# A graph network's one-hot build: edge differences on GpSimd, a re-cut load of the targets, identity and run bounds made on chip

## The reference

```python
def _L1_gnn_ref(x, edge_index, edge_attr, We, be, W1, b1, gamma, beta, W2, b2):
    msg = x[src] + (edge_attr @ We + be)
    agg = jax.ops.segment_sum(msg, dst, num_segments=x.shape[0])
    h = (agg + x) @ W1 + b1
    ...
    return h @ W2 + b2

edge_index = jnp.stack([src, dst])
x = _layernorm(x + _L0_gnn_ref(x, src, dst))
...
x = _layernorm(x + _L3_gnn_ref(x, edge_index, L3_gnn_W, L3_gnn_att_src, L3_gnn_att_dst, L3_gnn_bias))
```

## Time and profile before

| | us |
|---|---|
| median of 3 runs (1216.16 to 1217.31) | 1216.74 |
| profiled execution, its own time | 1217.54 |
| its span, first to last instruction | 1215.7 |
| PE busy in it | 1083.8 |
| DVE busy | 862.8 |
| ACT busy | 640.8 |
| POOL busy | 60.4 |

### The profile page before, as it was taken

One profiled execution on the slowest core, in us unless ns is written; L12 is line 12 of the kernel. 1 busy time (PEld: TensorE's weight loads), 2 busy tenths in 40 slices (PEclk: granted clock), 3 DMA queues, 4 the chain that ended last, 5 costly groups with the idle time before them and its releaser, 6 DMA issues.

```text
span 1215.7 us, 38923 instructions
## 1 busy us (share of the span) xinstructions
PE 1083.8 (89%) x16039; PEld 995.7 (82%) x16039; DVE 862.8 (71%) x2304; ACT 640.8 (53%) x1171; POOL 60.4 (5%) x109
## 2 busy tenths in 40 slices
PE   2766667679999999999998999599999999999997
PEld 1666656679999999999954999488989888898996
DVE  3999999975344434443631635788899899899997
ACT  1677777730000000000112402689899999999997
POOL 1000000001111111111000002000000000000000
PEclk8899999989999999999999799699999999999999
DMA  4555555410000000000000000000000000000000
GB/s 77 73 75 76 71 75 76 62 38 3 2 3 3 2 3 2 3 2 3 2 1 1 2 3 2 2 2 2 2 2 2 2 2 2 2 2 2 8 13 13
DMA packets 133045, 21.77 MB, mean 18 GB/s; under 512 B 132255, under 2 KB 132639, under 8 KB 132892
## 3 DMA queue, kind: packets, MB, share of 16 engines
q1 hardware_dynamic: 128920, 18.88, 10.3%
q10 hardware_dynamic: 3972, 0.68, 0.3%
HBM read 18.74 MB, written 0.80 MB: 16 GB/s over the span
## 4 chain that ended last, share of the span: by engine, by line
PE 55%; DVE 15%; ACT 6%; issue 3%; ACTq 0%; POOL 0%; DVEq 0%
PE bank L1927 33%; PE bank L2055 9%; DVE Mr L1537 5%; ACT Mr L922 4%; PE bank L2051 4%; PE bank L1870 3%; PE bank L1862 2%; PE bank L2115 1%; DVE F L1437 1%; DVE Mr L1544 1%; PE bank L1854 1%; DVE Nr L1500 1%; ACT F L862 1%; PE bank L1897 1%; ACT r L899 1%
## 5 line engine op out<-in xcount | busy, mean ns | idle before, releaser
L1927 PE MATMUL bank<-GH,C 128*128 128x128 f16 x7100 | 397.9, 219 | 0.0
L1927 PEld LDWEIGHTS bank<-GH,C 128*128 128x128 f16 x7100 | 396.9, 98 | 0.1
L2055 PE MATMUL bank<-F,Mr 128*128 128x260 f16 (+1 forms) x2538 | 317.4, 261 | 6.6 <-DVE Mr L1537 5.4
L2055 PEld LDWEIGHTS bank<-F,Mr 128*128 128x128 f16 x2538 | 214.6, 98 | 28.4 <-DVE Mr L1537 5.5
L1537 DVE TENSOR_TENSOR Mr<-Mr,C 128x640 f16<-128x640 f16 x461 | 210.8, 488 | 35.8 <-ACT Mr L922 31.8
L764 ACT ACTIVATE plo<-bank 128x256 f32<-128x256 f32 (+1 forms) x84 | 30.1, 360 | 362.9 <-PE bank L1927 346.7
L2051 PE MATMUL bank<-FN,C 128*128 128x130 f16 x1945 | 187.1, 220 | 5.3 <-DVE r L1446 4.9
L1745 PE MATMUL bank<-ohk,ohp 128*128 128x100 f16 (+3 forms) x1452 | 114.1, 214 | 81.9 <-ACT C L725 35.8
L1181 DVE TENSOR_TENSOR S<-bank,plo 128x256 f32<-128x256 f32 (+1 forms) x84 | 33.2, 395 | 209.3 <-ACT plo L764 209.2
L922 ACT ACTIVATE Mr<-cold,eaT 128x640 f16<-128x640 f32 x231 | 173.0, 819 | 11.4 <-PE bank L2055 10.5
L922 ACT ACTIVATE Mr<-eaT 128x640 f16<-128x640 f32 x230 | 172.4, 818 | 10.1 <-PE bank L2055 9.1
(11 more groups left out here) (263 smaller groups left out, 1006.5 us busy)
## 6 DMA issues: line engine op xcount, KB each, us to landing
raw<-in_edges_dram SPq DMA_DIRECT2D x237, 68.0 KB, 2.2
xs<-in_x_dram SPq DMA_DIRECT2D x1, 800.0 KB, 4.3
out_dram<-xs SPq DMA_DIRECT2D x4, 160.0 KB
dsts<-in_dst_dram SPq DMA_DIRECT2D x1, 465.0 KB
raw<-in_edges_dram ACTq DMA_DIRECT2D x5, 68.0 KB, 3.1
cold<-in_L_gnn_W_dram ACTq DMA_DIRECT2D x2, 64.0 KB
z<-in_L_gnn_att_src_dram SPq DMA_DIRECT2D x1, 128.0 KB, 2.8
z<-in_L_gnn_att_dst_dram SPq DMA_DIRECT2D x1, 128.0 KB, 3.0
```

Of the source, the lines that this page charges most:

```text
L1927: last = pe.matmul(bank[:, b, jj * 2 * D:(jj + 1) * 2 * D], C[:, t, (t0 + jj) * P:(t0 + jj + 1) * P], GH[:, par, t, :], start=t == 0 and j ...
L2055: return pe.matmul(bank[:, k, a_:z_], Mr[:, mi % RB, j * P:(j + 1) * P], F[:, t, a_:z_], start=start, stop=t == T - 1)
```

## The change

Five edits, all before the first hop. The differences `rest` leave DVE for a loop of their own on GpSimd, in the same order (this group's second half, then the next one's first), each waiting for the high parts (`s_hi`) alone. The 124 lines of targets are loaded as 64, 12 (SP) and 48 (ACT). The 17 parameter loads move from the front of ACT's queue to SP's, behind the loop that loads edges. `wlo` is made by two products of `bound` with a one on PE and a copy on DVE, and `ident` by a comparison on DVE. ACT runs a small activation at its front, and PE's first `begin` comes one row earlier.

```diff
@@ block.sync
-            sp.dma_start(dsts[1:RP, :], bass.AP(dst.tensor, dst.offset + (RC - 1) * ROW, [[RC * ROW, RP - 1], [1, (RC + 1) * ROW]])).then_inc(s_first, 16)
+            sp.dma_start(dsts[1:65, :], lines(1, 65)).then_inc(s_first, 16)
+            sp.dma_start(dsts[113:RP, :], lines(113, RP)).then_inc(s_first, 16)
             sp.dma_start(dsts[0:1, ROW:], dst.rearrange("(p c) -> p c", c=RC * ROW)[0:1, :]).then_inc(s_first, 16)
...
...
+                sp.dma_start(o_, i_).then_inc(s_w, 16)
+            for j_, i_ in enumerate((b1, gamma, beta)):
+                sp.dma_start(vecs[:, j_:j_ + 1], i_[:, None]).then_inc(s_w, 16)
             sp.wait_ge(s_lo, (G - 1) * 2)
@@ block.gpsimd
-            pool.iota(wlo[:], pattern=[[P * W, 2]], base=0, channel_multiplier=W, allow_small_or_imprecise_dtypes=True).then_inc(s_iota, 1)
-            pool.memset(ident, 0.0).then_inc(s_g, 1)
...
-            pool.affine_select(out=ident, in_=ident, compare_op=ALU.not_equal, fill=1.0, base=0, pattern=[[-1, P]], channel_multiplier=1).then_inc(s_cst, 1)
...
+            pool.wait_ge(s_ident, 1)
+            pool.tensor_copy(ident16, ident).then_inc(s_cst, 1)
...
+            def rest(i, k, u):
+
+                w0, w1_ = HALVES[u]
+                pool.wait_ge(s_hi, i * 4 + (k * 2 + u + 1))
+                pool.tensor_tensor(attrs(k % 2, w0, w1_), attrs(k % 2, w0, w1_), eahl[:, w0 * K:w1_ * K, 0:DE], ALU.subtract).then_inc(s_dif, 1)
+
+            rest(0, 0, 0)
+            with pool.Fori(0, G // 2 - 1) as i:
+                for par in range(2):
+                    rest(i, par, 1)
+                    rest(i, par + 1, 0)
+            rest(G // 2 - 1, 0, 1)
+            rest(G // 2 - 1, 1, 0)
+            rest(G // 2 - 1, 1, 1)
@@ block.scalar
...
-                act.dma_start(o_, i_).then_inc(s_w, 16)
-            for j_, i_ in enumerate((b1, gamma, beta)):
-                act.dma_start(vecs[:, j_:j_ + 1], i_[:, None]).then_inc(s_w, 16)
+            act.dma_start(dsts[65:113, :], lines(65, 113)).then_inc(s_first, 16)
+            act.wait_ge(s_ones, 1)
+            act.activation(small[0:1, 59:60], onesP[0:1, :], ACT.Copy)
@@ block.vector
-            v.wait_ge(s_first, 32)
+            v.sem_inc(s_bound, 1)
+            v.wait_ge(s_wlo, 1)
+            c.add(v.tensor_copy(wlo[:], bank[:, 2, 0:2]))
+            c.here()
+            v.tensor_scalar(ident, bound[:, 0:P], wlo[:, 0:1], None, ALU.is_equal).then_inc(s_ident, 1)
+            v.wait_ge(s_first, 64)
...
                 for u in range(NU):
                     build_unit(i, par, u)
-                    if u == 1:
-                        rest(i, par, 1)
-                    elif more and u == 2:
-                        rest(i, par + 1, 0)
                     if more and u:
                         keys(i, par + 1, u - 1)
@@ block.tensor
-                pe.wait_ge(s_cst, 2)
+                pe.wait_ge(s_ident, 1)
...
+            pe.matmul(bank[:, 2, 0:1], bound[0:1, 0:P], onesP[0:1, :], start=True, stop=True)
+            pe.matmul(bank[:, 2, 1:2], bound[0:1, P:2 * P], onesP[0:1, :], start=True, stop=True).then_inc(s_wlo, 1)
...
-                    if b == 1 and k == 2:
+                    if b == 1 and k == 1:
                         begin(0)
```

More of the change, by code:

```diff
@@ L270, in gnn_kernel @@
         s_first = sem("s_first")
+        s_bound = sem("s_bound")
+        s_wlo = sem("s_wlo")
+        s_ident = sem("s_ident")
         s_iota = sem("s_iota")
@@ L319, in steps, with lines @@
             return sum(by_act(h_, b_, t_) for h_ in range(H) for b_ in range(NG) for t_ in range(T) if (h_, b_, t_) <= (h, b, t))
+        def lines(a_, z_):
+            return bass.AP(dst.tensor, dst.offset + a_ * RC * ROW - ROW, [[RC * ROW, z_ - a_], [1, (RC + 1) * ROW]])
         def apart(h, b, t):
@@ L519, in _ @@
                         load_half(g, par, half)
+            for o_, i_ in ((weS[0:DE, :], We), (weS[DE:2 * DE, :], We), (weS[2 * DE:S1, :], be[None, :]), (w1[0:D, :], W1), (w1[D:P, :], W1), (w2[0:D, :], W2),
+                           (w2[D:S1, :], b2[None, :]), (wlr[:, 0:D], Wl), (wlr[:, D:2 * D], Wr), (wg[0:D], Wg.rearrange("k (h d) -> k h d", h=H)),
+                           (wg[D:P], Wg.rearrange("k (h d) -> k h d", h=H)),
+                           (biases[:, 0], bl[None, :].to_broadcast([P, D])), (biases[:, 1], br[None, :].to_broadcast([P, D])),
+                           (biases[:, 2], bias_g[None, :].to_broadcast([P, D]))):
+                sp.dma_start(o_, i_).then_inc(s_w, 16)
+            for j_, i_ in enumerate((b1, gamma, beta)):
+                sp.dma_start(vecs[:, j_:j_ + 1], i_[:, None]).then_inc(s_w, 16)
             sp.wait_ge(s_lo, (G - 1) * 2)
@@ L603, in _ @@
             pool.memset(eahl[:, :, 2 * DE:2 * DE + 1], 1.0).then_inc(s_iota, 1)
-            pool.wait_ge(s_iota, 11)
+            pool.wait_ge(s_iota, 10)
+            def rest(i, k, u):
[10 more added lines that the diff above has]
+            rest(G // 2 - 1, 1, 1)
             pool.wait_ge(s_x, 16)
@@ L701, in _ @@
                 act.dma_start(raw[:, 0, w0 + w], edges[bass.ds(s, SLOT), :].rearrange("(k p) c -> p k c", p=P)).then_inc(s_raw[0], 16)
-            act.wait_ge(s_iota, 11)
+            act.wait_ge(s_iota, 10)
             def positions(i, k):
@@ L972, in _ @@
                 v.tensor_scalar(starts_row[:, b * P:(b + 1) * P], bank[0:1, b, 0:P], -float(ROW), 0.0, ALU.add, ALU.max).then_inc(s_startrow, 1)
-            v.wait_ge(s_iota, 8)
+            v.wait_ge(s_iota, 7)
             def pairs(ap, n):
@@ L1002, in keys @@
                     along(ohj[:, par], iota_j[:], dl16[:]).then_inc(s_ohj, 1)
[L1004 to L1008, removed]
             def build_unit(i, par, u):
@@ L1036, in _ @@
                 keys(0, 0, step)
-            c.here()
-            rest(0, 0, 0)
             with v.Fori(0, G // 2 - 1) as i:
@@ L1357, in low_x @@
                 v.scalar_tensor_tensor(GH[:, 1, t0:t0 + n, D:2 * D], GH[:, 1, t0:t0 + n, 0:D], -LO, V[:, b % 2, 0:n, :], ALU.mult, ALU.add).then_inc(s_xl, 1)
-            v.wait_ge(s_cst, 4)
+            v.wait_ge(s_cst, 3)
             v.memset(own16, XS ** 0.5).then_inc(s_own, 1)
@@ L1715, in begin @@
                 pe.wait_ge(s_cnt, 2 * b + 2)
-                pe.wait_ge(s_cst, 2)
+                pe.wait_ge(s_ident, 1)
                 pe.matmul(bank[0:1, b, 0:P], cnt[:, b:b + 1], ident, start=True, stop=False)
                 pe.matmul(bank[0:1, b, 0:P], cnt[:, 2 + b:3 + b], ident, start=False, stop=True).then_inc(s_start, 1)
+            pe.wait_ge(s_ones, 1)
+            pe.wait_ge(s_bound, 1)
+            pe.matmul(bank[:, 2, 0:1], bound[0:1, 0:P], onesP[0:1, :], start=True, stop=True)
+            pe.matmul(bank[:, 2, 1:2], bound[0:1, P:2 * P], onesP[0:1, :], start=True, stop=True).then_inc(s_wlo, 1)
             pe.wait_ge(s_jump, 1)
@@ L1729, in _ @@
             begin(1)
-            pe.wait_ge(s_iota, 11)
-            pe.wait_ge(s_cst, 4)
+            pe.wait_ge(s_iota, 10)
+            pe.wait_ge(s_cst, 3)
             def window(i, par, w, first):
```

15 lines of the change are left out of this document (4 added, 11 removed).

## The result

| | us |
|---|---|
| after, median of 6 runs (1240.27 to 1250.89) | 1241.83 |
| before, median of 6 runs (1216.16 to 1217.81) | 1216.70 |
| ratio, with its 95% interval | 1.0212 (1.0196 to 1.0227) |
| profiled execution of after, its own time | 1250.89 |
| its span | 1249.1 |

The kernel is slower by 25.1 us; 28.0 had been forecast. The profiled execution is the longest of the six by 9 us (the other five lie from 1240.3 to 1241.9).

The account below looks back on a forecast made before the run. DVE was taken to bound the build loop: 189.8 us without the subtractions plus 71.0 of holds is 260.8, from 20.8 us, ending 28.0 later than before; 1216.7 + 28.0 = 1244.7 us, range 1226 to 1256 (63%).

Parts of the forecast that it names:

- DVE's loop without `rest`: Build loop on DVE: 225.4 us less 34.8 for the subtractions and 0.8 for waiting on ACT's high part, 189.8 us.
- The hold: Build loop: each GpSimd subtraction stops DVE for its whole span less 0.07 us; 71.0 us charged in all.
- my two pairs of rows: Earlier GpSimd operations giving the subtraction spans: 2.13 ns an element, 3.37 us a group; or 1.5 ns, 2.71, the lower bound.
- The waits: Build loop: no term for GpSimd's late turns in the sum; a few late handovers only in the 1256 us high end.
- The rival in which GpSimd does not get its turn: Build loop: DVE's next operation wins; ACT, PE, DVE wait 0.5 to 1.5 us per group, 1256 to 1280 us; 11%.
- the one case in the earlier trace: Hops: GpSimd's copy came while L1367 ran on DVE and went in before L1369, which stood directly behind.
- The start: Ahead of the loop: targets 4.2 us earlier, `begin` 0.5, keys without high-part wait and subtraction 2.7; loop starts at 20.8 us.
- The parameter loads: On SP behind the last window load they fill idle time; x in time even 4 us late; no effect.
- The signs I named: L1018 and L1020 means up by 3.2 us a group, group near 11.9 us, SP waiting over 29 us, hops unchanged.
- a TensorE clock below 0.97: Named as a sign that would be wrong: a clock under the loop's 0.97, since PE is busy for a smaller share.
- The even rival: Build loop: shorter holds; sign turns at 1.05 us a hold, 1.3 to 1.4 ns an element; 1210 to 1226 us; 9%.

Follow-up runs that it names:

- the kernels that leave one form on DVE: After, with only the 640-element subtractions on GpSimd and the 768 on DVE: 1228.41 us; the reverse: 1234.86 us.
- the kernel with all 44 meeting DVE: After, plus a DVE wait behind each unit of one-hots for its own last one-hot to complete, 66 times: 1250.71 us.
- parameter loads alone: The kernel before with only its 17 parameter loads moved from ACT's queue to SP's, behind the edge loads: 1216.62 us.
- the old start: The kernel before with only the 44 differences moved to GpSimd's own loop, the start left as it was: 1250.75 us.
- the new start alone: After with the differences back on DVE in their old places, the other edits kept: 1212.11 us.

## Why the prediction was right, by its steps

**DVE's loop without `rest`: 189.8 us.** Right within 1.2 us: 191.0 in after by the account, and 190.4 and 190.9 in the kernels that leave one form on DVE, with its 0.88 or 0.74 us each taken off.

**The hold.** The mechanism was right and shown three ways: it appears with every subtraction that meets DVE at work, it is gone with the read, and it scales with the elements. Its size was too large. I charged 3.37 us a group less 0.14; the holds are 1.43 + 1.19 = 2.62. Two terms failed. The spans, extrapolated from 64 and 256 elements at 2.13 ns an element, are 1.61 and 1.37 us (2.98 a group, not 3.37, between my two pairs of rows). And 0.18 us of each is hidden (1.61 - 1.43, 1.37 - 1.19), not 0.07, more than the 0.14 I gave as its bound. With both measured, 44 holds are 22 x 2.62 = 57.6 us instead of 71.0; the kernel with all 44 meeting DVE shows 56.5, seven of them shortened by a stop. In after 36 of the 44 met DVE at work, 47.4 us; the eight others ran while it was idle.

The Trainium skill (SBUF — State Buffer, Who interferes with whom) gives this lock for the whole instruction; the runs agree, with 1.84 to 1.87 ns an element at four sizes and no one-hot held by a GpSimd instruction that only writes. By the Trainium skill's figure for 2048 elements (GPSIMD Engine Reference, Elementwise — side-by-side cycle accounting) the spans were estimated at 1.69 and 1.41 us; 1.61 and 1.37 were measured, so that estimate was nearer than mine.

**The waits: nothing, in the forecast.** This term was missing. The rival in which GpSimd does not get its turn came true in part: it asks, up to 11 of DVE's operations go first, and ACT, PE and DVE stand one behind the other, 28.0 us of idle time in the profiled run. I had argued from the one case in the earlier trace rows, a turn won at the first boundary; here 21 of 44 were won at the first or second, seven met a standing DVE, and 16 missed, the last of them until DVE stood still. The rival had 11 to 33 us on top of the forecast's hold, and the waits lie in that span; but the smaller hold paid for most of it: 260.8 + 1.2 for the rest of the loop, -23.6 for the hold (47.4 for 71.0) and +28.0 for the waits are the 266.4 us. In the median run, if start, end and the 1.8 us around the span were the same, the loop was 1241.8 - 1.8 - 962.2 - 20.4 = 257.4 us. The right total of the forecast owes something to two errors of opposite sign.

**The start: -7.4 us.** -7.83 measured. The targets came at 4.96 (4.7 forecast). GpSimd's iota was forecast to hold the old search back, and the new identity and `wlo` were to remove that; in truth it comes earlier by itself with the new load, so the parts of the start beside the load bring little: 1212.11 against 1212.63 us. Their first one-hot is 1.8 us earlier (22.58 for 24.42), of which the median keeps 0.5; the profiled spans behind the loop differ by 0.7 us the other way (962.1 and 961.4), and no run tells whether that is chance. Of the 7.8 us the time sees less if DVE keeps its differences: with the first subtraction and its wait back, the first one-hot is at 22.58 and the gain 4.6 us.

**The parameter loads: nothing.** Confirmed alone, 1216.62.

**The signs I named.** The mean of L1040 rose from 509 ns (L1018) to 565, the group took 266.4 / 22 = 12.1 us (11.9 forecast), SP waited longer (63.6 us for 29.0), the hops stayed. The mean of `ohp` didn't rise (1176 ns before, 1124 after): the held ones are the operation that happens to follow. I had also said that a TensorE clock below 0.97 would be wrong, and it was 0.82. By itself it doesn't stop DVE: the kernel with a stop after each unit has 0.79 in its loop, and DVE waits 0.5 us for PE there. How much of after's 27.7 us of waits for PE it lengthened, no run separates.

**A sum that was off.** The even rival's hold of 1.05 us is 1.49 ns an element over the mean size of 704, not 1.3 to 1.4. Nothing else rests on it; the measured hold is 1.31 us on the mean, above it.

**Not settled.** What decides the turn. In after a request at 215.38 us, with 0.32 us left of the second of three-window one-hots, won at its end; one at 251.53, in the same operation with 0.34 us left, was passed by. A missed turn is served later, mostly at the first `ohk` of the unit of four windows or at `keys`, while other operations with the same kind of wait on a semaphore go by ahead of it; for half the elements the same places come up. The Trainium skill (SBUF — State Buffer, Who interferes with whom) says that whoever issues first gets the shared ports. That doesn't describe these rows: at 116.13 the record of GpSimd's begins before those of five DVE operations that went ahead of it. I can give no rule in its place. That it takes a gap of DVE was tried with the 66 stops and is refuted, since 37 of its turns were won without one; what does decide stays open.

## What to carry to other kernels

Ask of an idle engine first what it shares with the busy one: an elementwise step moved from a saturated VectorE to GpSimd that reads SBUF costs VectorE its whole reading time, here 2.62 us for the 1.62 it had taken itself, unless GpSimd's part only writes. Give such a step slack behind it, since its turn may come several microseconds late. And look at the parts of a change one by one: here the re-cut load by itself gave 4.1 of the start's 4.6 us, and the loss in the loop hid it.

## What the runs showed of the hardware

- A reading GpSimd operation and a DVE operation exclude each other for 1.86 ns an element and partition (float32, two inputs). That hits one-input operations also: `ki`, a TENSOR_SCALAR of 128x44 int32 that takes 0.20 us, took 1.37. A GpSimd memset of the same 768 elements (0.75 us) held no one-hot, but the one-input `woff` (128x44 float32) until its own end, twice, by 0.08 and 0.20 us.
- GpSimd may be passed by. Its operation counts as running from its request, so its span has the wait in it: 1.61 to 6.98 us for the same 768 elements, with up to 11 DVE operations ahead of it. The DVE operation that is held counts as busy. Neither shows in the idle columns.
- A stopped VectorE does not help: with DVE waiting on the subtraction's semaphore, its idle time is 67.9 us for 28.0, against the 40.0 us of holds that this removed.
- One DMA of 124 lines used about four engines' worth of time, an estimate from the earlier trace rows; as 64, 12 and 48 lines the same targets are there 3.6 us earlier (5.27 for 8.87). The DMA view's slices of 0.45 us (tenths that the 16 engines are busy, 0 to 18 us) show it with the parameter loads out of the way in both: first the one DMA (parameter loads alone), then the re-cut load (after).

```profile
DMA  0000222122223222100000000000000000000001
```

```profile
DMA  0000999930000000000000000000029969999999
```

- GpSimd's first iota, which nothing in the program delays, ran at 10.97 us in the kernel before, 10.79 with the parameter loads moved and 10.41 with the old start, and between 8.30 and 9.20 in the kernels with the re-cut load (8.44 in after, 9.20 with the new start alone). It comes earlier with the re-cut load; why was not tried.
